# Expert rows: from ScalarE's DMA queue back into SyncE's, ahead of the same expert's weights

## The reference, cut to what matters

```python
E, K, H, I, CAP = 64, 8, 512, 192, 128
w, sel = jax.lax.top_k(probs, K)                 # 8 of 64 experts for each token
xin = zeros((E, CAP + 1, H)).at[eid, slot].set(x[tok])   # up to 128 tokens per expert
h = silu(einsum('ech,ehi->eci', inp, wg)) * einsum('ech,ehi->eci', inp, wu)
out = einsum('eci,eih->ech', h, wd)
y = zeros((T, H)).at[tok].add(out * weight)      # added back to the token's row
```

## Time and profile before

| | us |
|---|---|
| median of three runs | 1737.85 (1732.64 to 1740.98) |
| the profiled execution, its own time | 1744.28 |
| its span in the trace | 1742.4 |
| granted TensorE clock, mean | 0.94 |
| expert loop, first rows asked for to last add landed | about 1356 to 1718 |

### The profile page before, as it was taken

How to read it: one execution, slowest core, us unless ns; L and a number is a source line. 1 busy time by engine, 2 the same in 40 slices (tenths; PEclk the granted TensorE clock), 3 DMA queues, 4 the chain that set the end, 5 groups by cost and what they waited for, 6 DMA issues and landing times. The chain is left out here.

```text
span 1742.4 us, 19092 instructions
## 1 busy us (share of the span) xinstructions
PE 1506.9 (86%) x5792; PEld 1038.0 (60%) x5792; DVE 1062.9 (61%) x1591; ACT 583.2 (33%) x1034; POOL 794.6 (46%) x491
## 2 busy tenths in 40 slices
PE   6989966899948899988999899999991799998992
PEld 2444323577736677766887787778771455554551
DVE  4887688887898987889988746452553122222220
ACT  4434633344534335343433322121210232222220
POOL 3467853354744445634644326662376232222222
PEclk8999988999969999999999999999995899999996
DMA  6899663356644677766655468997760799999987
GB/s 202 251 280 277 194 217 132 101 156 196 199 140 149 201 221 222 216 192 225 187 183 169 145 201 305 351 317 227 227 191 25 227 329 317 311 306 301 307 211 126
DMA packets 193541, 380.41 MB, mean 218 GB/s; under 512 B 20994, under 2 KB 95106, under 8 KB 192944
## 3 DMA queue, kind: packets, MB, share of 16 engines
q1 hardware_dynamic: 165360, 322.89, 59.8%
q0 software_dynamic: 20032, 39.92, 9.7%
q10 hardware_dynamic: 8064, 16.55, 2.8%
HBM read 301.65 MB, written 124.35 MB: 244 GB/s over the span
## 5 line engine op out<-in xcount | busy, mean ns | idle before, releaser
L1453 POOL TENSOR_TENSOR y<-y,hc 128x2048 f32<-128x2048 f32 x64 | 293.3, 4582 | 250.3 <-DVE hc L1295 250.3
L590 PE MATMUL bank<-tokT,ring 128*128 128x512 f32 x768 | 307.9, 401 | 12.9 <-DVE xall L1150 6.9
L1277 DVE TENSOR_TENSOR_SCAN bx<-bank,state,bx 128x512 f32<-128x512 f32 x256 | 312.6, 1267 | 0.8
L592 PE MATMUL bank<-tokT,ring 128*128 128x512 f32 x768 | 302.3, 394 | 0.0
L591 PE MATMUL bank<-tokT,ring 128*128 128x512 f32 x768 | 302.2, 393 | 0.0
L940 ACT ACTIVATE bank<-dl,an 128x512 f32<-128x512 f32 x256 | 171.0, 684 | 330.4 <-DVE bx L1277 330.3
L1459 POOL TENSOR_TENSOR act<-th,act 128x512 fp32r<-128x512 f32 x96 | 126.4, 1316 | 269.6 <-ACT act L864 269.1
L819 PE MATMUL bank<-wgu,xeT 128*128 128x384 f32 x512 | 181.0, 498 | 0.0
L590 PEld LDWEIGHTS bank<-tokT,ring 128*128 128x128 f32 x768 | 146.2, 190 | 49.2 <-issue 17.6
L602 PE MATMUL bank<-ring,act 128*128 128x512 f32 x360 | 147.6, 410 | 22.6 <-DVE th L1139 17.3
L592 PEld LDWEIGHTS bank<-tokT,ring 128*128 128x128 f32 x768 | 146.0, 190 | 32.1
(11 more groups left out here) (147 smaller groups left out, 2007.9 us busy)
## 6 DMA issues: line engine op xcount, KB each, us to landing
ring<-w_all SPq DMA_DIRECT2D x288, 512.0 KB
wgu<-wgu_in SPq DMA_DIRECT2D x64, 768.0 KB
wde<-wd_in SPq DMA_DIRECT2D x64, 384.0 KB
slots<-empty_in SPq DMA_DIRECT2D x16, 1154.0 KB, 8.7
w_all<-staged_u SPq DMA_DIRECT2D x64, 256.0 KB, 3.2
xe<-slots ACTq DMA_DIRECT2D x56, 288.5 KB
w_all<-fst SPq DMA_DIRECT2D x48, 256.0 KB, 3.7
w_all<-staged_d SPq DMA_DIRECT2D x32, 256.0 KB, 3.7
```

The lines of the kernel that those rows point to most:

```text
L590: nc.tensor.matmul(b[:, :], w[:, k, 0, :], x[:, 0, k, :], start=(k == 0), stop=False)
L592: last = nc.tensor.matmul(b[:, :], w[:, k, 1, :], x[:, 0, k, :], start=False, stop=(k == KT - 1))
L1277: nc.vector.tensor_tensor_scan(bx[:, k, :], dA[k % 2][:, :], bx[:, k, :], state[:, k, n:n + 1], ALU.mult, ALU.add).then_inc(S_sc, 1)
L1453: nc.gpsimd.tensor_tensor(y[c % 2][:, :, :], y[c % 2][:, :, :], hc[:, :, :], ALU.add).then_inc(S_ya, 1)
```

## The change

The rows of expert e + 8 are no longer asked for by ACT. SP asks for them, in the same queue as the weights and directly ahead of the `wgu` of the same expert. SP now waits for two things ahead of both: that gate and up of e are done (`S_gm`, as before; moved out of `load_weights`), and that DVE has read `wsc` and `tok` of e out of the rows buffer (`S_ws`, which ACT waited for). `next_rows` and its call are gone from ACT. The first eight experts' rows were already asked for by SP and stay so.

```diff
                     def load_weights(e, i):
-                        if not isinstance(e, int):
-                            sp.wait_ge(S_gm, e - DEEP + 1)
                         sp.dma_start(wgu[i][:, :, :], ...).then_inc(S_ew[i], 16)
                         if not isinstance(e, int):
                             sp.wait_ge(S_y, e - DEEP + 1)
                         sp.dma_start(wde[i][:, :, :], ...).then_inc(S_ew[i], 16)
...
                     with sp.Fori(0, E // DEEP - 1) as q:
                         for i in range(DEEP):
-                            load_weights(DEEP * q + i + DEEP, i)
+                            e = DEEP * q + i
+                            sp.wait_ge(S_gm, e + 1)
+                            sp.wait_ge(S_ws, e + 1)
+                            load_rows(e + DEEP, i)
+                            load_weights(e + DEEP, i)
...
-                    def next_rows(e, slot):
-
-                        if not isinstance(e, int) or e + DEEP < E:
-                            act.wait_ge(S_ws, e + 1)
-                            nc.scalar.dma_start(xe[:, slot, :], a["slots"][ds((e + DEEP) * P, P), :]).then_inc(S_xe[slot], 16)
-
...
                         if not first:
-                            next_rows(DEEP * q + i - 1, (i - 1) % DEEP)
                             down(*previous(q, i))
```

## The result

| | before | after |
|---|---|---|
| median, five executions each | 1737.85 us | 1750.69 us |
| ratio, 95% interval | | 1.0085 (1.0055 to 1.0115) |
| the profiled execution | 1744.28 us | 1746.63 us |

A forecast was written before the change was run, and what follows sets the result against it. The chain of adds was taken to bound the loop. Adds' 16.2 us gain, capped at 14.6 by the loads, less one late-load stall of 2.4, made 12 us off the median 1737.85: 1726 us, range 1711 to 1751.

The forecast's parts named there:

- the chain of adds: Expert loop: two side-by-side chains of adds, each waiting for a landing, set the pace at 5.57 us an expert.
- The turns: DMA queues alternate packet by packet; without ACT's queue, an add's nine turns fall from 3.48 to 2.7 us.
- I take 0.77: Adds in the loop: each lands 0.77 us sooner, after 9.63 us, within bounds of 0 and 5.5 us gained.
- if landings stay above 10.2 us: Sign of a miss: adds' issue to landing staying above 10.2 us, where about 9.6 was forecast, means no gain.
- the 16.2 us: Expert loop: adds' pace falls by 0.38 us to 5.19 us an expert, saving 16.2 us over 42 experts.
- The loads at 307 GB/s minus the adds: Loop loads get 256.5 GB/s, 5.75 us an expert; the last load lands 4 us later, by 1689.6.
- The lead of the loads: End of the loop: the last load, landed by 1685.5, left 18.7 us unused before the last gate-and-up.
- SP's queue alone does not fill the engines: Slower rival: outside the adds' turns SP's loads run at 234 to 279 GB/s, 13 us slower, 1751 us; chance 0.23.
- Its other half: Slower rival's sum: the loss arises outside the adds' turns, where SP's queue falls below 279 GB/s.
- The parts at nothing: ACT's saved issue and wait, SP's added issue and wait for S_ws, and rows sharing SP's queue: each costs nothing.
- Nothing, as long as the backlog stays under some 30 us: Rows behind SP's other loads: no cost, as data is wanted 35 us after it is asked for.
- Several issuers: No-gain rival's skill rule: queues share 16 DMA engines, several issuers save only issue time; 1736 us, chance 0.27.

The follow-up runs named there:

- wait_only: The kernel before, with the wait for S_ws added in SP's queue ahead of wgu, rows still asked for by ACT: ratio 0.9996 to the kernel before.
- wde_act: The changed kernel with the loop's wde loads moved to ACT's queue, rows and wgu left in SP's: 1714.07 us, ratio 0.9840 to the kernel before.
- after_again: The changed kernel, no edit, measured again: median 1747.70 us beside 1740.82 for the kernel before, ratio 1.0000.
- short_pe_after: The changed kernel with small stores in place of the adds and gate-and-up cut to a quarter: ratio 0.9890 to the kernel before.
- short_pe: Small stores for adds, gate-and-up cut to a quarter, in the changed kernel, kernel before and wde_act: ratios 0.9890, 0.9846 and 0.9600 to the kernel before.
- wde_rows_act: The kernel before, rows in ACT's queue, with the loop's wde loads moved to ACT's queue too: ratio 0.9951 to the kernel before.

## Why the prediction was wrong

**That the chain of adds set the pace before.** Right for the long stretch: with the adds nearly gone the loop fell from 361 to 331.5 us.

**The turns.** Right to the digit, in the one stretch looked at: nine turns were forecast at 2.7 us, and two adds' packets took 5.4.

**"I take 0.77": that a landing gains what its turns gain.** This step failed. The turns gave 0.77 us, the landing only 0.2 (10.4 to 10.2). The rest of the time, which no row split and which I held constant, took back most of it. Even the 0.2 is within the spread: from 1446 to 1600 the median landing was 10.4, 10.5 and 10.1 us in the two traces of before and in `wait_only`, and 10.2 in both of the changed kernel. My sign of a miss was "if landings stay above 10.2 us"; they stayed at that edge. The adds' pace stayed where it was, 42 in 234 us, so the 16.2 us never existed. `wde_act` shows the wrong idea in it: there a third queue took its turns as before, and adds came each 5.13 us, faster than in either kernel. A landing does not follow from the number of queues alone.

**The loads at 307 GB/s minus the adds.** This step failed too, and it turned the sign. I took the total rate as given and let queues only divide it. It depends on how the loads are spread over queues: 307 fell to 296 (287 in the second trace). In the same terms, I let every packet keep its time. Over the stretch before, a packet held a DMA engine 0.229 us in SP's queue and 0.097 in ACT's, which for 256 and 144 of an expert is 0.181 in the mean; afterwards it was 0.189. Loads came at 249 GB/s, 1.475 / 0.249 = 5.92 us an expert where 5.75 was forecast and 5.65 measured before. Over the 41.4 experts that is 11 us more than before in this stretch alone, and at the end the last rows landed at 1701.5, where the last load was forecast by 1689.6. The lead of the loads, 18.7 us at the end before, was spent already from about 1600 on, and from there PE waits for rows.

**The rival that came true.** It was the slower one, "SP's queue alone does not fill the engines", at 1751 us; 1750.69 was measured. I gave it 0.23, and weighed against it a stretch of 4.5 us at 379 GB/s, with nothing else going on, over the 234 GB/s seen inside the loop. The short burst was the weaker witness. The experiments show its mechanism without the adds (266 against 286 GB/s) and alone (261).

Its other half, that the loss sits outside the adds' turns, the traces bear out only in part, so the exact hit is partly luck. During two adds' packets all queues together moved 2.22 MB in 6.9 us before, 322 GB/s, and 1.63 MB in 5.4 us afterwards, 302: the turns themselves became slower. If all adds of the long stretch moved so, the rest of it ran at about 284 GB/s before and 291 after, above the 279 under which that sum sees a loss, and at 273 in `after_again`, below it (estimates: the add packets of the stretch, 5917, 6049 and 5966, at those of the earlier trace rows or of the window above, and the rest of its bytes).

**The parts at nothing.** The wait for `S_ws` costs nothing (`wait_only`). "Nothing, as long as the backlog stays under some 30 us" held in its letter, a load of rows took 21.9 us, and yet PE waited for rows: the backlog was not only in the DMA queue. SP's issues began to take up to 5.4 us, and the last rows were asked for 14.5 us after the step that allowed it (1665.4 to 1679.90). I did not test whether this costs by itself; as the queue's share stayed at 100.3% while it happened in `short_pe_after`, it looks like a sign of the full queue and not a second cause.

**Several issuers.** The queues' taking turns held. Moving one load of 0.39 MB per expert from SP's queue to ACT's raised 261 GB/s to 329 in the `short_pe` runs, and made the changed kernel 1.6% faster than the one before. ACT's issue of it takes 0.32 us, at no cost to PE, which stayed busy 153.75 of 154 us. The Trainium skill (Trainium Kernel Development and Optimization, Key Constraints) says that issuing from several engines only saves issue time; by these rates that does not fit this case.

## What to carry to other kernels

When the DMA engines read as fully busy, look at GB/s beside the share: busy engines moved 261 or 329 GB/s here, by the arrangement of queues alone. And compare more than one trace: the kernel before moved 307 and 309 GB/s in two executions, and with a wait added that costs nothing 319. If several load streams share one hardware queue, try giving one large one to the other queue, on an engine that can stand a blocked issue. And when the last load of a loop lands long before its last use, count that gap: it hides a slower load rate until it is used up.

## What the runs showed of the hardware

One hardware load queue, fed with packets of 2.3 to 6 KB without a pause, moved 261 GB/s over 134 us while its share of the 16 engines was 100.3% (`short_pe_after`); two moved 278 or 329, depending on which loads went where. Worked out from the same lines, a packet of 3.7 KB in the mean held a DMA engine 0.232 us with all loads in one queue, and one of 3.5 to 3.8 KB 0.183 to 0.185 us with `wde` in the other. Why the engines are busy longer per byte with one queue is open. An issue of a DMA from SP, 0.33 us, took up to 5.4 us in the changed kernel once the packets asked for and not yet moved came to about three experts' loads (my count from the trace), and from ACT up to 2.8 us, with ACT's own work behind it (`wde_rows_act`).
